# ScalarE rounds to int16 and VectorE takes over one turned tile in four, in the second phase of a linear-attention and quantised-FFN layer

## The reference

```python
x = x + _L0_attn_ref(_layernorm(x), qkv_w, qkv_b, out_w, out_b)     # causal linear attention, 16 heads
x = x + _L0_ffn_ref(_layernorm(x), weight_int8, weight_scale, bias)

def _L0_ffn_ref(x, weight_int8, weight_scale, bias):
    x2 = x.reshape(-1, K)
    x_scale = max(abs(x2).max() / 127.0, 1e-5)          # one scale for all of x
    x_int8 = clip(round(x2 / x_scale), -128, 127)
    acc_i32 = x_int8 @ weight_int8.T
    return acc_i32 * x_scale * weight_scale.T + bias
```

## Time and profile before

| | |
|---|---|
| median of 3 runs | 1107.83 us |
| the profiled execution | 1108.21 us |
| its span | 1106.5 us |
| mean granted TensorE clock | 0.994 |
| PE busy over the span | 97% |
| POOL busy | 79% |
| VectorE busy | 73% |
| ScalarE busy | 63% |

### The profile page before, as it was taken

How to read it: one execution, slowest core, us unless ns; L and a number is a source line. 1 busy time by engine, 2 the same in 40 slices (tenths; PEclk the granted TensorE clock), 3 DMA queues, 4 the chain that set the end, 5 groups by cost and what they waited for, 6 DMA issues and landing times. The chain is left out here.

```text
span 1106.5 us, 30806 instructions
## 1 busy us (share of the span) xinstructions
PE 1068.3 (97%) x11591; PEld 789.6 (71%) x11604; DVE 805.3 (73%) x1540; ACT 701.1 (63%) x1258; POOL 875.0 (79%) x1087
## 2 busy tenths in 40 slices
PE   5899999999999999999999999999999999986998
PEld 3677777777778777777778777877777777762443
DVE  6687676777776777677677677667767766687887
ACT  6666656666566656656666666565665566635996
POOL 3387887788887888888778877778888878883999
PEclk9999999999999999999999999999999999997999
DMA  7223333333333333333333333333333333243994
GB/s 266 61 56 97 97 87 97 87 81 86 94 87 90 85 90 94 97 89 86 96 78 90 87 92 85 90 87 90 97 97 87 87 87 87 49 127 119 366 354 189
DMA packets 74982, 120.80 MB, mean 109 GB/s; under 512 B 16465, under 2 KB 16977, under 8 KB 74834
## 3 DMA queue, kind: packets, MB, share of 16 engines
q1 hardware_dynamic: 74304, 118.29, 36.5%
q10 hardware_dynamic: 530, 0.54, 0.2%
HBM read 36.97 MB, written 31.46 MB: 62 GB/s over the span
## 5 line engine op out<-in xcount | busy, mean ns | idle before, releaser
L598 PE MATMUL unit<-xt_hi,w_hi 128*128 128x256 f16 x1000 | 273.6, 274 | 4.8 <-ACT relu L925 1.9
L598 PE MATMUL unit<-xt_hi,w_lo 128*128 128x256 f16 x1000 | 273.7, 274 | 0.0
L598 PE MATMUL unit<-xt_lo,w_hi 128*128 128x256 f16 x1000 | 273.7, 274 | 0.0
L925 ACT ACTIVATE relu<-unit,qk_bias_scaled 128x256 f32<-128x256 f32 x250 | 117.8, 471 | 178.6 <-PE unit L598 175.6
L1232 DVE SCALAR_TENSOR_TENSOR x_ring<-sc,x_ring 128x512 f16<-128x512 f32 x256 | 175.3, 686 | 52.6 <-ACT x_ring L967 49.0
L441 POOL TENSOR_TENSOR qk_lo<-f_t,qk_hi 128x512 f16<-128x512 f32 x128 | 148.7, 1163 | 52.1 <-ACT qk_hi L944 52.1
L967 ACT ACTIVATE x_ring<-sc 128x512 f16<-128x512 f32 x256 | 148.1, 591 | 63.4 <-PE sc L647 63.4
L458 POOL TENSOR_SCALAR_AFFINE_SELECT x_ring<-x_ring 128x512 f16<-128x512 f16 x256 | 164.3, 642 | 25.5 <-DVE x_ring L1232 24.7
L460 POOL TENSOR_SCALAR_AFFINE_SELECT x_ring<-x_ring 128x512 f16<-128x512 f16 x256 | 168.4, 658 | 0.0
L598 PEld LDWEIGHTS unit<-xt_hi,w_hi 128*128 128x128 f16 x1000 | 98.0, 98 | 24.5 <-ACT relu L925 2.9
L598 PEld LDWEIGHTS unit<-xt_lo,w_hi 128*128 128x128 f16 x1000 | 98.1, 98 | 16.9
(11 more groups left out here) (210 smaller groups left out, 2750.6 us busy)
## 6 DMA issues: line engine op xcount, KB each, us to landing
stack<-qk_hi SPq DMA_DIRECT2D x504, 64.0 KB, 2.0
xs<-x SPq DMA_DIRECT2D x64, 256.0 KB, 2.7
stack<-qk_lo SPq DMA_DIRECT2D x256, 64.0 KB, 2.0
out<-res SPq DMA_DIRECT2D x64, 256.0 KB, 3.6
x_spill<-xs SPq DMA_DIRECT2D x56, 256.0 KB, 2.2
x_ring<-x_spill SPq DMA_DIRECT2D x56, 256.0 KB, 4.4
stack<-qkv_wt SPq DMA_DIRECT2D x6, 512.0 KB, 8.2
x_ring<-out_wt SPq DMA_DIRECT2D x1, 1024.0 KB, 12.1
```

What stands on the lines that cost most here:

```text
L598: mm = pe.matmul(dst[:, 0:GT], wp[:, k, f:f + P], xp[:, g % 2, k, :], start=(n == 0), stop=(n == len(terms) - 1))
L925: act.activation(relu[:, i % 4, :], src[:, 0:GT], ACT.Relu, bias=qk_bias_scaled[:, f:f + 1]).then_inc(qk_done, 1)
```

## The change

ScalarE writes `u` as int16, so the conversion on its output does the rounding. VectorE's `quantise` becomes a `tensor_copy` that widens int16 to bf16. The evictions of turned tiles are shared out: every tile with t % 4 == 3 is copied from `tp` to `xq_t` by VectorE (position: behind `quantise` of the tile two later, ahead of `scale_back`), the other three by ScalarE as before. The semaphore `xq_t_ready` becomes two, one for each engine, and TensorE waits for that of the tile. ScalarE's fetch of a round's scales goes; it reads `affine` directly.

```diff
+            def on_vector(t):
+                return t % 4 == 3
+
+            def wait_turned(eng, i, t):
+                tile = i * RING + t
+                if on_vector(t):
+                    eng.wait_ge(turned_dve, tile // 4 + 1)
+                else:
+                    eng.wait_ge(turned_act, tile + 1 - (tile + 1) // 4)
...
-            u = buf(two, "u", [P, DEEP, E])
+            u = buf(two, "u", [P, DEEP, E], I16)
...
# TensorE: transpose waits for tile t - DEEP, multiply for tile t
-                        pe.wait_ge(xq_t_ready, seen(i, t - DEEP))
+                        wait_turned(pe, i, t - DEEP)
...
-                    pe.wait_ge(xq_t_ready, seen(i, t))
+                    wait_turned(pe, i, t)
...
# ScalarE
-                def fetch(i, first):
-                    if first:
-                        return
-                    act.wait_ge(u_ready, seen(i, -1))
-                    src = affine[:, i] ...
-                    act.activation(cur[:, :, :], src, ACT.Copy).then_inc(cur_ready, 1)
-                    act.wait_ge(cur_ready, i)
...
-                    own = affine[:, 0] if first else cur
+                    own = affine[:, i]
...
-                        if not (first and t < OUT_LAG):
+                        if not (first and t < OUT_LAG) and not on_vector(t - OUT_LAG):
                             turn_out(i, t - OUT_LAG, first)
...
-                for t in range(RING - OUT_LAG, RING):
-                    turn_out(ROUNDS - 1, t, False)
+                turn_out(ROUNDS - 1, RING - OUT_LAG, False)
...
# VectorE
-                    dve.tensor_scalar(xq[:, t % DEEP, :], u[:, t % DEEP, :], ROUND_MAGIC, ROUND_MAGIC, ALU.add, ALU.subtract
-                                      ).then_inc(xq_ready, 1)
+                    dve.tensor_copy(xq[:, t % DEEP, :], u[:, t % DEEP, :]).then_inc(xq_ready, 1)
+
+                def turn_out(i, t, first):
+                    dve.wait_ge(tp_ready, seen(i, t))
+                    if not (first and t < DEEP):
+                        dve.wait_ge(acc_ready, seen(i, t - DEEP))
+                    dve.tensor_copy(xq_t[:, t % DEEP, :, :], tp[t % DEEP][:, 0:EC, :]).then_inc(turned_dve, 1)
...
-                BACK = 3
+                TURN, BACK = 2, 3
...
+                        if on_vector(t - TURN) and not (first and t < TURN):
+                            turn_out(i, t - TURN, first)
                         if not (first and t < BACK):
                             scale_back(i, t - BACK, first)
...
-                for t in range(RING - BACK, RING):
+                scale_back(ROUNDS - 1, RING - BACK, False)
+                turn_out(ROUNDS - 1, RING - 1, False)
+                for t in range(RING - BACK + 1, RING):
                     scale_back(ROUNDS - 1, t, False)
```

More of the change, by code:

```diff
@@ L16 @@
 I32 = mybir.dt.int32
+I16 = mybir.dt.int16
 P = 128
@@ L26 @@
 EXPONENT_BITS = 0x7F800000
-ROUND_MAGIC = 12582912.0
 def build(nc, x, qkv_wt, qkv_b, qk_b, out_wt, out_b, ffn_wt, ffn_scale, ffn_bias, out):
@@ L1572, in build @@
             affine = buf(two, "affine", [P, ROUNDS, 2, RING])
-            cur = buf(two, "cur", [P, 2, RING])
             dq = buf(two, "dq", [P, E])
@@ L1594, in build @@
             dq_ready = sem("dq_ready")
-            cur_ready = sem("cur_ready")
             u_ready = sem("u_ready")
@@ L1599, in build @@
             tp_ready = sem("tp_ready")
-            xq_t_ready = sem("xq_t_ready")
+            turned_act = sem("turned_by_act")
+            turned_dve = sem("turned_by_dve")
             acc_ready = sem("acc_ready")
@@ L1710, in _ @@
                 act.wait_ge(affine_ready, 2)
-                def fetch(i, first):
-                    if first:
-                        return
-                    act.wait_ge(u_ready, seen(i, -1))
-                    src = affine[:, i] if isinstance(i, int) else affine[:, bass.ds(i, 1)].rearrange("p a s c -> p (a s) c")
-                    act.activation(cur[:, :, :], src, ACT.Copy).then_inc(cur_ready, 1)
-                    act.wait_ge(cur_ready, i)
                 def scale_tile(i, t, first, last):
@@ L1736, in turn_out @@
                         act.wait_ge(acc_ready, seen(i, t - DEEP))
-                    act.activation(xq_t[:, t % DEEP, :, :], tp[t % DEEP][:, 0:EC, :], ACT.Copy).then_inc(xq_t_ready, 1)
+                    act.activation(xq_t[:, t % DEEP, :, :], tp[t % DEEP][:, 0:EC, :], ACT.Copy).then_inc(turned_act, 1)
                 OUT_LAG = 2
                 def body(i, first, last):
-                    fetch(i, first)
                     for t in range(RING):
                         scale_tile(i, t, first, last)
-                        if not (first and t < OUT_LAG):
+                        if not (first and t < OUT_LAG) and not on_vector(t - OUT_LAG):
                             turn_out(i, t - OUT_LAG, first)
                 rounds(act, body)
-                for t in range(RING - OUT_LAG, RING):
-                    turn_out(ROUNDS - 1, t, False)
+                turn_out(ROUNDS - 1, RING - OUT_LAG, False)
             @block2.vector
```

## The result

| | before | after |
|---|---|---|
| median | 1108.12 us (4 runs) | 1100.69 us (4 runs, 1099.09 to 1101.98) |
| ratio | 1 | 0.9932 [0.9913, 0.9951] |
| median, timed again | 1109.22 us (8 runs) | 1103.20 us (5 runs, 1102.61 to 1105.80) |
| ratio, timed again | 1 | 0.9946 [0.9931, 0.9960] |
| span of the profiled execution | 1106.5 us | 1097.4 us |

The change makes the kernel faster: by 7.5 us (5.4 to 9.6) in the first comparison and by 6.0 us (4.4 to 7.7) in the second. The span overstates it: the first phase, which is the same in both, ended 1.84 us earlier in the profiled execution of after (VectorE's first instruction of the second phase, `ve_all`, starts at 999.92, before at 1001.76). One execution of the kernel of experiment 7 ran at a mean granted clock of 0.946 (1125.53 us) and is left out of its median.

The account below looks back on a forecast made before the run. The prediction took the exclusion between VectorE's `xq` and POOL's add as the bound: 58 tiles × (1.418 − 1.315) = 6.0 us, less 15 × 0.01 for turns, gave 5.8, so 1102.0 us from 1107.83; range 1100.8 to 1106.2.

Parts of the forecast that it names:

- Lock-step of `xq` and POOL's add: Second phase, steady state: VectorE's `xq` and POOL's add exclude each other, one each per tile, setting 1.418 us a tile.
- `xq` at 0.28 alone: VectorE, second phase: reading int16 shortens `xq` from 0.42 to 0.28 us when nothing runs beside it.
- PE the next bound at 1.315, slack 0.14: Second phase: PE sets 1.315 us a tile, with `xq` early enough for the transposes by 0.14 us.
- 58 tiles × 0.103 = 6.0: Second phase's steady tiles: the pace falls from 1.418 to 1.315 us over 58 tiles, gaining 6.0 us.
- The turn at 0.41 just in time: VectorE's eviction of every fourth turned tile, taken at 0.42 us: PE's multiply loses 0.01 us each, 15 times.
- The tail costs 0: End of second phase: turn 63 on VectorE delays the last multiply by 0.2 us, hidden inside POOL's 0.4; cost 0.
- The first two tiles run before the lock-step: Beginning of second phase: these two tiles were left out of the 58 that gain.
- The POOL bound: Rival, second phase: the add's halt only halves, so POOL stays the bound at 1.335 us a tile; 1103.0 us, chance 0.13.
- the turn at 0.69: Rival: VectorE's eviction from PSUM takes 0.69 us, giving back 4.1 of the 6.0 us; 1106.0 us, chance 0.12.
- the copy that isn't faster: Rival: int16 leaves `xq` at 0.42 us alone, the pace staying at 1.418 a tile; 1107.8 us, chance 0.08.
- the DMA that can't follow: Rival: the 40 tiles with reloads stay at 1.418 us and only 19 gain, 2.0 us; 1105.8 us, chance 0.03.
- the slower case: Rival: VectorE's turn of 0.69 us ahead of `y`, with `xq` no faster, stalls PE; 1111 us, chance 0.05.

Follow-up runs that it names:

- experiment 7: After without VectorE's share of turned tiles, plus 12 PE matmuls whose result nobody reads during the wait for the global maximum: 1099.81 us, ratio 0.9929 to before.
- experiment 4: Before, with POOL copying `y` into `res` in place of adding the second residual: 1101.91 us (one run).
- 1: After with the int16 copy alone, all 64 turned tiles staying on ScalarE: 1103.1 us, ratio 0.993 to before.
- 2: After with sharing alone, `u` staying float32 and rounded by two additions on VectorE: 1108.3 us, ratio 0.9995 to before.

## Why the prediction was right or wrong

The forecast was 1102.0 us from 1107.83, a gain of 5.8. The measured median, 1100.69, lies 0.1 us below the lower end of the range. The mechanism was right. What failed is a term of the sum that was put at zero, the phase's beginning. Step by step:

- **Lock-step of `xq` and POOL's add.** Right, and shown from both sides: shorten POOL's operation (4) or halve `xq`'s stream (1), and the pace is PE's.
- **`xq` at 0.28 alone.** Right (0.282; 0.33 in place, 0.31 forecast).
- **PE the next bound at 1.315, slack 0.14.** PE needs 1.303 (75.55/58 in 4), so 0.01 less than I took from the rows; the slack in the tile shown measures 0.10 (0.16, of which 0.06 is latency).
- **58 tiles × 0.103 = 6.0.** 82.12 − 76.13 (the mean of three profiles) is 5.99. PE's smaller need gives 6.4 without sharing (82.12 − 75.74); sharing took 0.4 back.
- **The turn at 0.41 just in time.** Right, 0.41 and multiplies 1.30 to 1.31 apart. That it costs nothing was nearly right: 0.3 to 0.4 in all, not 0.15, about 0.02 a turn in place of 0.01, and 0.1 at each of two places.
- **ScalarE's relief worth nothing.** Right: with 48 turns on ScalarE in place of 64 nothing is gained, with either form of `xq` (1, 2).
- **DMA follows.** Right: 396 GB/s.
- **The tail costs 0.** It gained 0.2 (9.87 to 9.64).
- **"The first two tiles run before the lock-step", counted as no gain: this step failed.** In the execution first profiled the second `y` starts 1.09 us earlier in the phase (11.66 against 12.75), which with the 5.95 of the 58 tiles and 0.2 of the tail makes 7.26. The sum had only the 5.8. Two things lie in the 1.09. The first tiles' `xq` are shorter by 0.13 each, and the first `y` starts 0.4 to 0.8 earlier in three profiles of after (10.43, 10.50 and 10.09, against 10.90 to 10.92 in all four with a source of four bytes). The other is a term that I didn't price at all, though the trace of before had it: PE's clock is at 0.50 there, and when it rises, from 9.4 to 12.7 us into the phase, moves the second `y` between 11.3 and 13.2. At a like rise the second `y` comes only 0.2 to 0.3 earlier with int16 (12.58 against 12.75 at 12.0 and 11.9; 12.84 against 13.00 and 13.15 at 12.5, 12.4 and 12.7). So most of the 1.09 was luck: the second profile of after gained nothing there (12.84), the third 1.4 (11.33).
- **The range's lower end** took in 0.5 us of scatter. The same first phase ended between 999.9 and 1006.5 us in thirteen profiles, and the second phase moves by 1.4 with the clock (97.12 to 98.54 in three profiles of after). Medians of the same kernel came out as 1100.69 and 1103.20. The mechanism and the size of the steady part were right; the range was too narrow below for medians that scatter so. Timed again, the gain was 6.0.

Of the rivals, none happened. The prediction's chances for "same" add up to 0.17 (0.06, 0.08 and 0.03), not 0.15; nothing hangs on it. The POOL bound came close (1.281 against 1.303), the turn at 0.69, the copy that isn't faster, the DMA that can't follow and the slower case are excluded by the rows above.

## What to carry to other kernels

When two engines are both full at the same pace and neither needs it alone, look for instructions of the two that stretch each other: the same instruction short at the phase's beginning and long in its steady state gives them away. Shorten the part that excludes the other engine (here 16-bit in place of 32-bit data in one copy) before moving work between engines; the move here cost 0.3 to 0.4 us and bought nothing. A busy share near 100% isn't a bound by itself: ScalarE with all the turns showed 19.92 of 20 us and nobody waited for it. And before a phase in which PE has stood idle, look at its granted clock.

## What the runs showed of the hardware

- ScalarE rounds to int16 or int32 on its output at the speed of float32: 0.804, 0.803 and 0.803 us for 512 elements with two operands per row.
- A VectorE copy of 512 bf16 elements out of PSUM takes 0.41 us, a float32 operation from PSUM 0.69. The Trainium skill (VectorE: DVE Perf Modes, why PSUM operands drop a tier) has two elements a cycle for the 16-bit form. The trace agrees: 0.41 is 0.02 above the 0.39 us that is my estimate from that page's errata table (120 + 512/2 cycles).
- The two-input float32 add on POOL takes 1.24 us alone, from start to start (1.26 by its record). A copy takes 0.61 alone (the last four and the 48th of experiment 4), and 0.65 to 0.74 when it begins before an `xq` has ended.
- PE's granted clock fell to 0.50 (1.2 GHz) in the pause between the phases, at different times in different executions (from 1.8 us before `ve_all` to 0.8 behind it, with the first phase's last matmul ending 3.8 before it). With PE busy again from 6.0 us, it rose at different times in executions of the same kernel, up to 3 us apart (9.5 and 12.5 in after).
- One gap stands ahead of POOL's 48th operation, the last of the third round, in every kernel here. It is 0.17 to 0.34 us in those changed from after (POOL's timeline above: 47 adds, then the gap) and 0.12 in before (1080.58 to 1080.70, inside the row of 55); in experiment 4 the idle time there is 0.91 in place of 0.62. With int16 one `y` behind it comes 1.50 after the last in place of 1.30, and two `xq` behind it take 0.62 and 0.60 in after. Before and experiment 4 lose nothing by it in `y`. Nothing in the profile releases it. Its cause is open.
